# Gated cross-attention with a ternary FFN: dummy matmuls, a new VectorE order and ternary pairs spread over slots 0 to 4

## What is computed

```python
def _ternary_weight(w, group_size):               # groups of 64
    wb = w.astype(jnp.bfloat16)
    wg = wb.reshape(-1, group_size)
    scale = jnp.clip(jnp.mean(jnp.abs(wg), axis=-1, keepdims=True), 1e-08, None)
    q = jnp.clip(jnp.round(wg / scale), -1.0, 1.0)
    qs = (q * scale).reshape(w.shape).astype(w.dtype)
    return w + jax.lax.stop_gradient(qs - w)
...
h = jnp.square(jax.nn.relu(jnp.einsum('bsd,hd->bsh', x, w1)))
...
x = x + jnp.tanh(g_xattn[0]) * _L0_xattn_ref(_layernorm(x), ctx_2048, ...)
x = x + jnp.tanh(g_ffn[0]) * _L0_ffn_ref(_layernorm(x), L0_ffn_W_fc, L0_ffn_W_proj)
```

## Time and profile before

| What | us |
|---|---|
| Median of 3 runs (1038.61 to 1042.93) | 1040.46 |
| The profiled execution | 1042.64 |
| Its span | 1040.8 |
| Start to the scores of slot 0 | 39.37 |
| Slots 0 to 4, from scores to scores | 28.45, 36.09, 38.65, 45.35, 32.86 |
| Slot 5 to the end | 820.03 |

### The profile page before, as it was taken

How to read it: one execution, slowest core, us unless ns; L and a number is a source line. 1 busy time by engine, 2 the same in 40 slices (tenths; PEclk the granted TensorE clock), 3 DMA queues, 4 the chain that set the end, 5 groups by cost and what they waited for, 6 DMA issues and landing times.

```text
span 1040.8 us, 26171 instructions
## 1 busy us (share of the span) xinstructions
PE 937.2 (90%) x10001; PEld 580.4 (56%) x10102; DVE 676.1 (65%) x1363; ACT 702.3 (67%) x1232; POOL 555.7 (53%) x616
## 2 busy tenths in 40 slices
PE   3557648899999999999999999999999999999987
PEld 1333325566566656656665666666566656666663
DVE  7897888766666666666666666666666666665410
ACT  2777576467677776767766777777676767776653
POOL 1232244447665555656576655656565766555454
PEclk9688689999999999999999999999999999999998
DMA  7625222233223332233323232332323222312010
GB/s 292 168 56 140 75 71 52 52 72 72 45 60 67 67 72 66 68 62 72 73 62 52 63 67 67 72 71 64 62 72 73 67 48 62 72 42 52 22 31 20
DMA packets 150797, 74.06 MB, mean 71 GB/s; under 512 B 136208, under 2 KB 136208, under 8 KB 149136
## 3 DMA queue, kind: packets, MB, share of 16 engines
q1 hardware_dynamic: 150672, 72.38, 29.6%
...
## 4 chain that ended last, share of the span: by engine, by line
PE 71%; DVE 10%; issue 8%; ACT 7%; DMA 2%; POOL 1%; DVEq 0%; SPq 0%; another core or an unknown queue 0%; ACTq 0%; POOLq 0%
PE mix_ps L429 9%; PE score_ps L384 9%; PE score_ps L386 9%; PE score_ps L385 9%; PE up_pair L415 9%; PE up_pair L416 8%; PE mix_ps L428 7%; PE score_ps L500 2%; PE score_ps L477 2%; DVE w L1139 1%; ACT big L765 1%; DVE m_rows L1158 1%; DVE q_raw L1079 1%; DMA ft<-x_rows 1%; ACT q_rows L726 1%
## 5 line engine op out<-in xcount | busy, mean ns | idle before, releaser
L415 PE MATMUL up_pair<-ft,w 128*128 128x256 f16 x960 | 217.4, 274 | 2.8 <-DMA ft<-x_rows 1.3
L416 PE MATMUL up_pair<-ft,w 128*128 128x256 f16 x960 | 217.3, 273 | 0.0
L1524 POOL TENSOR_TENSOR k_weighted<-k_raw,qk_norm 128x512 f32<-128x512 f32 x32 | 41.8, 1306 | 272.5 <-DVE k_raw L1085 270.9
L429 PE MATMUL mix_ps<-w,big 128*128 128x512 bf16 x464 | 176.3, 380 | 10.6 <-issue 9.1
L1538 POOL TENSOR_TENSOR big<-h_sb,big 128x512 f16<-128x512 f32 x128 | 148.2, 1158 | 44.6 <-ACT big L765 21.3
L1548 POOL TENSOR_TENSOR hh_sum<-hh_sum,hh_sb 128x512 f32<-128x512 f32 x112 | 149.0, 1331 | 9.3 <-ACT hh_sb L781 9.3
L997 DVE TENSOR_TENSOR p_lo<-score_ps,p_hi 128x512 f16<-128x512 f32 x128 | 88.5, 691 | 93.5 <-ACT p_hi L712 93.5
L428 PE MATMUL mix_ps<-w,big 128*128 128x512 bf16 x379 | 143.9, 380 | 2.9 <-POOL big L1538 2.9
L830 ACT ACTIVATE score_ps<-score_ps,log_p,exp_scale 128x512 f32<-128x512 f32 x128 | 95.5, 746 | 58.0 <-PE score_ps L503 58.0
L759 ACT ACTIVATE h_sb<-up_pair,relu_scale 128x512 f32<-128x512 f32 x120 | 81.4, 678 | 60.4 <-PE up_pair L416 60.4
L415 PEld LDWEIGHTS up_pair<-ft,w 128*128 128x128 bf16 x960 | 94.0, 98 | 26.4 <-DMA ft<-x_rows 5.9
...
## 6 DMA issues: line engine op xcount, KB each, us to landing
...
big<-in_w_fc_t SPq DMA_DIRECT2D x4, 1024.0 KB, 5.2
big<-in_w_proj_t SPq DMA_DIRECT2D x4, 1024.0 KB, 5.4
big<-in_wq_t SPq DMA_DIRECT2D x1, 1024.0 KB, 7.8
big<-in_wk_t SPq DMA_DIRECT2D x1, 1024.0 KB, 9.9
big<-in_wv_t SPq DMA_DIRECT2D x1, 1024.0 KB, 10.3
```

The source lines that it names most:

```text
L415: nc.tensor.matmul(dst[:, half], w, ft[i][:, c, :], start=(c == 0), stop=False)
L416: last = nc.tensor.matmul(dst[:, half], w, ft[i][:, C + c, :], start=False, stop=(c == C - 1))
L429: last = nc.tensor.matmul(dst[:, :], ht_lo[i][:, row], w2[:, m, :], start=False, stop=(m == M - 1))
```

## The change

**TensorE.** `warm(n)` issues n matmuls of 384 columns into a free part of `mix_ps`; nobody reads them. 14 stand ahead of `tops_t`, 4 behind it (ahead of `scores_t`) and 6 or 8 behind `scores_t`, in slots 0 to 3 (none behind `scores_t` in slot 3). They wait for nothing of their own. The pairs' group sums move: pair 0 into the setup, in slots 0 and 1 none between the queries and the values, in slots 2 and 3 six halves a slot in place of eight. In slot 2 `ffn_up` pieces 1 and 2 come one place later.

**Pairs.** Group sums and clips of pairs 0 to 3 stand in slot 0, of 4 to 7 in slot 1, of 8 to 10 in slot 2, of 11 to 13 in slot 3, and of 14 and 15 in slot 4, which gets its own list, `join_slot`. A third `t_scale` (the unused `out_sb[1]`) makes `TD = 3`, so that products may lag: those of pairs 2 and 3 go to slot 1, of pair 7 to slot 2.

**VectorE.** Slots 0 to 4 have new lists: fewer pair operations stand ahead of `score_tops`; `next_context` (the context's maximum) moves between the last two `probs_lo`.

**Slot 4.** `ffn_down` of tile 0 is split: blocks 4 to 11 behind the scores, 12 to 15 behind the projections of tile 5, and the values follow them. Values, attention and the output projection come last, with no FFN piece between.

**ScalarE, SyncE, GpSimd.** ScalarE's lists follow; `raw_scale(0)` comes ahead of pair 1's Abs in the setup, `ternary` of 2 behind `tops(0)`. The loads of the ternary source of w2, in number b = 4 to 7, go from slots 1, 1, 2, 2 to slots 1, 2, 2, 3. In slots 1 to 3 GpSimd's `rows_plus_constant` waits for the first row maximum of its slot.

```diff
-    PAIRS = (4, 4, 4, 4)
-    FIRST = (0, 4, 8, 12)
-    RAW = FIRST[2]
-    TD = 2
+    RAW = NU // 2
+    TD = 3
...
+        warm_rows = top_pick[:, :, :].rearrange("p u k -> p (u k)")[:, 0:384]
...
+        t_scale = [sb(f"t_scale{i}", [P, 1024], BF16) for i in range(2)] + [out_sb[1][:, :].bitcast(BF16)]
@@ TensorE
+            def warm(n):
+                for _ in range(n):
+                    nc.tensor.matmul(mix_ps[:, 0:384], group_mean[:, :], warm_rows, start=True, stop=True)
             def early_slot(t):
                 scores(t)
                 if t == 0:
-                    pe.wait_ge(ctx_top_ready, 2)
-                ternary_pair(p)
+                    pe.wait_ge(attn_set, 6)
+                    ternary_pair(1)
+                else:
+                    ternary_pair(4)
+                warm(14)
                 tops_t(t)
+                warm(4)
                 scores_t(t)
-                ternary_pair(p + 1)
+                if t == 1:
+                    ternary_pair(5)
+                warm(6)
                 next_keys(t)
                 next_queries(t)
-                ternary_pair(p + 2)
                 pe.wait_ge(mt_ready, t + 1)
                 values(t)
                 attention_rows(t)
+                ternary_pair(p + 2)
                 next_values(t)
...
+            def join_slot(t):
+                scores(t)
+                ternary_half(2 * NU - 4)
+                ffn_down(0, range(4, 12), mix_ps)
+                tops_t(t)
+                ternary_half(2 * NU - 3)
+                square_sums(0)
+                scores_t(t)
+                pe.wait_ge(hms_ready, 1)
+                ffn_up(g, j, 0, up_ps, 1)
+                next_keys(t)
+                ternary_half(2 * NU - 2)
+                ffn_up(g, j, 1, up_ps, 1)
+                next_queries(t)
+                ternary_half(2 * NU - 1)
+                ffn_up(g, j, 2, up_ps, 1)
+                next_values(t)
+                ffn_down(0, range(12, 16), mix_ps)
+                pe.wait_ge(mt_ready, t + 1)
+                pe.wait_ge(out_ready, 1)
+                values(t)
+                attention_rows(t)
+                project_out(t)
+                next_context(t)
+                ffn_up(g, j, 3, up_ps, 1)
+                ffn_down(1, range(0, 4), mix_ps)
@@ VectorE, slot 1
+            def second_slot():
+                score_tops(1)
+                ternary_products(2)
+                tops_t(1)
...
@@ GpSimd
                 if not first:
+                    if t < J:
+                        pool.wait_ge(top_ready, 4 * t + 1)
                     rows_plus_constant(t, j)
```

More of the change, by code:

```diff
@@ L691, in _ @@
                 middle_slot(t)
-            for t in range(J, NT):
+            join_slot(J)
+            for t in range(J + 1, NT):
                 slot(t)
@@ new lines, in middle_slot @@
+                q_hi(t + 1)
+                if t == 2:
+                    ternary_sign(10)
+                    squares(g, j, 0)
+                    relu(g, j, 1, up_ps)
+                attention_hi(t)
+                if t == 2:
+                    halves(g, j, 1)
+                    squares(g, j, 1)
+                    ternary(11)
+                else:
+                    ternary(14)
+                    relu(g, j, 2, up_ps)
+                    squares(g, j, 1)
+                v_hi_of(t + 1)
```

308 lines of the change are left out of this document (192 added, 116 removed).

## The result

The changed kernel takes **1033.84 us** (median of 6 runs, 1031.77 to 1036.70); the kernel before, in runs beside it, 1041.62. The ratio is 0.9932, 95% interval 0.9906 to 0.9959: faster by 0.7%, where 1.6% was forecast. The time lies 9.8 us above the forecast of 1024.0 and 1.3 above the upper end of the range. The profiled execution took 1031.77, its span 1030.0.

The account below looks back on a forecast made before the run. VectorE's order, not capacity, was taken to bound slots 0 to 4, its waits leaving TensorE at 1.2 GHz; TensorE bounds the rest. Slot terms of -19.2 plus 2.7 allowance gave -16.5 from 1040.46: 1024.0 us, range 1016.5 to 1032.5.

Parts of the forecast that it names:

- The +0.7 of slot 0: Slot 0: the 14 dummies start cold behind pair 1 and take its place, costing 0.7 us.
- The dummies' term: Slots 0 to 3: clock terms of 11.25 us won by dummies holding the clock, less 0.7 in slot 0.
- they are hidden: Slots 0 to 3: the 14 dummies take 2.3 to 4.5 us within the wait for the row maxima.
- Rival 1: Slots 0 to 3: dummies don't hold the clock, or only after a slow start; 8 us lost, 1032; chance 0.14.
- Its own estimate: Slot 4: group sums, `ffn_out`, bare attention tail and first relu cost 5.1 us, less 1.1 for earlier maxima: +3.9.
- The maxima come 1.1 earlier: Slot 4: the row maxima come 1.1 us earlier than before, set against 5.1 us of costs.
- rival 4: Moved pair products on VectorE collide with GpSimd, 1.07 us each; 22 more caught gives 1047; chance 0.03.
- ScalarE's order: Every slot: small things a walk forgets, allowed 0.5 us a slot; 2.7 with the slow start after slot 2's gap.
- up to 1.0 a slot: Slots 1 to 3: GpSimd's new wait moves its sum from beside VectorE's product, worth up to 1.0 us each.
- Slot 4 over 40: Slot 4: a length over 40 us, against about 37 expected, would show the prediction wrong.
- Rival 3: Waits move, don't go: slots 2, 3 win only the clock's 2.1, 6.6; slot 4 pays 8; 1034 to 1038; chance 0.07.
- within 1 us of 820: Slot 5 to the end: bound by TensorE and untouched, its length stays within 1 us of 820.

Follow-up runs that it names:

- e1: The changed kernel without its dummy matmuls, all else equal: 1039.62 us, ratio 0.9998 to the kernel before.
- e0: The changed kernel run again, unchanged: 1033.19 us, ratio 0.9929 to the kernel before.
- e3: The changed kernel with dummies in slot 4 too: 1030.89 us, ratio 0.9905 to the kernel before.
- e10: The changed kernel without any dummy, with slot 2's query norm first on GpSimd and pair 13's products behind slot 4's `m_sb`: 1033.29 us.
- e2: The kernel before, lists and pairs unchanged, with dummies added in slots 0 to 3: 1036.34 us, ratio 0.9962.
- e8: The changed kernel with pair 13's products behind slot 4's `m_sb` and FFN blocks 10 and 11 behind the transposed scores: 1029.05 us.
- e9: The changed kernel with three edits (dummies in slot 4, slot 2's query norm first on GpSimd, pair 13's products later): 1028.54 us, again 1027.49.
- e13: The three edits of e9, plus pair 6's products behind slot 2's maxima and `m_sb`: 1027.08 us, again 1027.98.
- e4: The changed kernel with GpSimd's query norm ahead of its first `hidden_lo` in slot 2: 1030.48 us, ratio 0.9902.
- e5: The changed kernel without GpSimd's wait for the first row maximum in slots 1 to 3: 1034.29 us, ratio 0.9934.

## Why the prediction was wrong, and where it was right

Three kernels split each slot's term in two: order (e1 less before, what it does to the clock included) and dummies (after less e1). The +0.7 of slot 0 is a price of the dummies and stands with them:

| Slot | order, forecast | measured | dummies, forecast | measured | sum, forecast | measured |
|---|---|---|---|---|---|---|
| 0 | 0 | -0.4 | -1.8 | -0.2 | -1.8 | -0.6 |
| 1 | -6.55 | -6.5 | -3.15 | -1.0 | -9.7 | -7.5 |
| 2 | +0.65 | +4.2 | -2.75 | -1.9 | -2.1 | +2.3 |
| 3 | -6.65 | -10.2 | -2.85 | +0.8 | -9.5 | -9.5 |
| 4 | +3.9 | +13.2 | 0 | -2.3 | +3.9 | +10.9 |
| all | -8.65 | +0.3 | -10.55 | -4.7 | -19.2 | -4.3 |

**The dummies' term was mis-sized.** In slots 0 to 3 they were worth 2.4 us by these profiles, 5.1 with the second one of the changed kernel (e0) and 1.1 with that of e3, whose lists for these slots are the same; 10.55 was forecast. With slot 4's 2.3 or 3.1 the first two make 4.7 to 8.2, and whole runs say 6.9 (0.66%). Where it went, in us after the slot's scores, without dummies (e1) and with them (after):

| Slot | L488 | transposed scores | values | next scores |
|---|---|---|---|---|
| 0 | 4.37, 7.10 | 5.69, 8.23 | 17.17, 16.94 | 28.10, 27.89 |
| 1 | 6.16, 6.16 | 7.50, 7.50 | 19.42, 16.10 | 29.56, 28.55 |
| 2 | 9.36, 10.93 | 11.88, 12.30 | 25.85, 23.26 | 42.88, 40.97 |
| 3 | 8.15, 7.63 | 9.71, 10.47 | 21.83, 22.59 | 35.12, 35.88 |

The step that failed is "they are hidden", and with it the clock given back in full in each slot:

- Slot 0: from L488 to the values the faster products win 3.0 us, more than the 2.5 forecast. But the 14 dummies, cold, hold L488 up by 2.7 us (2.1 in e0), not 0.7.
- Slot 1: nothing stands in the way, and the values come 3.3 us earlier for a forecast of 3.15. Then the clock falls at 87 us, for the next sums of a pair and the next values' projection, and 2.3 of it is lost again. In e0 it doesn't fall, and the slot takes the forecast 27.0. Without dummies the clock can also come up earlier: in e10 the values come at 16.86, and slot 1 takes 29.32.
- Slot 2: 2.6 at the values, 1.9 at the end, for 2.75.
- Slot 3: nothing for 2.85. The 4 dummies behind L488 run at the low clock, the transposed scores start 2.84 us behind L488 where e1 has 1.56, and run at 1.2 GHz all the same; the key products ran at the full clock before as well.

So the time that transposed scores and key products lose at 1.2 GHz was on the path, as forecast, in slots 0 to 2; what the forecast missed is what the dummies cost there and where the clock falls next. e2 shows the same in the old lists. Rival 1 named this in part (a slow start, 8 us of the clock terms lost: 8.2 were, or 5.5 with e0). Its sign, a mean clock under 0.85, couldn't show it.

**Slot 4 was the largest miss**, 7.0 us over. Its own estimate counted waits one by one and left out two things. (a) The clock there was taken as kept; the moved work opened waits of 1.5, 1.5 and 2.4 us, and the clock fell: 3.7 us (2.9 against e0), shown by e3. (b) "The maxima come 1.1 earlier": they start 5.52 us after the scores against 4.37 in the kernel before (192.28, the scores at 187.91), 1.15 later, since the three operations of pair 13 met GpSimd's `hidden_lo` and `hidden_sum`: 2.4 us longer than alone, and 3.3 were had back in e8, which takes the two products away from there. This is rival 4's mechanism at one place. Over slots 0 to 4, 12 of the 48 pair products took over 0.8 us, where 17 did before (the prediction had some 14). Of (a) and (b) together 4.7 to 5.9 us were had back (e9, e13), not 7.0. The rest, tail and group sums, was near: at the full clock and without pair 13 slot 4 takes 37.9 (e13), against 36.8 forecast.

**Slot 2** was 4.4 over. Its front was as told, gap and slow dummies included; the dummies cost 0.4 us at the transposed scores. Most of the loss was on a queue that I had not walked, GpSimd's: "ScalarE's order" went into an allowance that no row gave. 3.2 us (2.4 against e0), shown by e4; of the other 1.2, 0.8 is the dummies' term above.

**Right**: slot 3 (35.9 against 35.85, though through two errors that cancel), the order's part of slot 1 to 0.1 us, the wait for the transposition in front of slot 2's scores gone, waits ahead of L488 of 2.3 and 2.8 us in slots 1 and 3 (under 4), GpSimd's new wait free on its own queue and worth 0.9 in slot 2 (e5; "up to 1.0 a slot"), slot 5 to slot 30 within 1.5 us (742.15 against 743.62). Of its signs, a clock of 0.9 or more came in slot 1 (0.94) and was just missed in slots 2 and 3 (0.89). Slot 4 over 40 was the sign of being wrong, and it came. Rival 3 (waits move and don't go, 1034 to 1038) had the result at its edge with a chance of 0.07; it deserved far more, since slot 4's tail was its case already. Its sum doesn't add up, for 2.1 and 6.6 are 8.7 and not 6, and slot 2's 2.1 has the clock in it.

The text on the end, "within 1 us of 820", was wrong through the last 75 us, whose length varies by 5.

The version with three edits beats both kernels: 1.05 and 1.26% under the kernel before in two series, against the changed kernel's 0.7%.
